# Cross attention 1: who copies the turned weights out of PSUM

## The reference, cut to what matters

```python
x = _layernorm(x + _L1_attn_ref(x, ...))        # state = tanh(state * exp(A) + Bu[t]), 1024 steps; y = states @ C_w.T + ...
x = _layernorm(x + _L1_xattn_ref(x, ctx_768, Wq, Wk, Wv, Wo, bo))

def _L1_xattn_ref(x, context, Wq, Wk, Wv, Wo, bo):   # 16 heads of 64, 77 keys per sequence
    q, k, v = (x @ Wq), (context @ Wk), (context @ Wv)          # split into heads
    attn = softmax(einsum('bqhd,bkhd->bhqk', q, k) / sqrt(64))
    return einsum('bhqk,bkhd->bqhd', attn, v).reshape(B, Nq, 1024) @ Wo + bo
```

## Time and profile before

| what | us |
|---|---|
| runs | 2312.34, 2312.98, 2318.16; median 2312.98 |
| the profiled execution's own time | 2315.36 |
| its span | 2313.6 |
| PE busy over the span | 1758.1 (76%) |
| DVE busy | 1782.5 (77%) |
| ACT busy | 1333.4 (58%) |
| POOL busy | 847.5 (37%) |
| the 11-transpose groups L1675 of the stage | first at 1644.4, last at 1990.1 |

### The profile page before, as it was taken

One profiled execution on the slowest core, in us unless ns is written; L12 is line 12 of the kernel. 1 busy time (PEld: TensorE's weight loads), 2 busy tenths in 40 slices (PEclk: granted clock), 3 DMA queues, 4 the chain that ended last, 5 costly groups with the idle time before them and its releaser, 6 DMA issues. The chain is left out here.

```text
span 2313.6 us, 36269 instructions
## 1 busy us (share of the span) xinstructions
PE 1758.1 (76%) x12104; PEld 1097.3 (47%) x12104; DVE 1782.5 (77%) x4542; ACT 1333.4 (58%) x3347; POOL 847.5 (37%) x983
## 2 busy tenths in 40 slices
PE   8939999999968777775666666665899999556564
PEld 4503333333336566664444554434577667433333
DVE  4668888888626888885888888845578787599997
ACT  1204666666733344342078888899999992144443
POOL 2420000000007768753333333300575775323232
PEclk9957999999967989896777777767899999866766
DMA  2001111111020010000000000010000000000000
GB/s 79 19 21 29 30 30 30 30 28 29 12 63 15 12 31 13 12 6 19 1 19 1 1 1 1 1 35 23 1 19 1 1 1 1 30 12 16 14 15 18
DMA packets 42807, 41.54 MB, mean 18 GB/s; under 512 B 16054, under 2 KB 34670, under 8 KB 42622
## 3 DMA queue, kind: packets, MB, share of 16 engines
q1 hardware_dynamic: 42622, 39.23, 6.4%
HBM read 22.03 MB, written 4.19 MB: 11 GB/s over the span
## 5 line engine op out<-in xcount | busy, mean ns | idle before, releaser
L763 ACT ACTIVATE ST<-ST,aexp 128x1 f32<-128x1 f32 x2046 | 581.9, 384 | 2.0 <-PEq L57 2.0
L597 ACT ACTIVATE PT<-PS 128x512 f32<-128x512 f32 x576 | 309.8, 597 | 219.5 <-PE PS L482 188.6
L558 DVE CUSTOM_DVE_ANT_0 junk<-PS,maskw 128x128 bf16<-128x128 f32 (+3 forms) x512 | 226.5, 486 | 33.8 <-PE PS L459 33.8
L459 PE MATMUL PS<-KT,QT 48*128 48x512 bf16 (+3 forms) x768 | 190.1, 351 | 54.1 <-DMA QT<-QS 33.0
L561 DVE TENSOR_REDUCE MX<-PS 128x1 f32<-128x512 f32 x256 | 164.6, 685 | 27.7 <-PE PS L459 24.9
L501 PE MATMUL PS<-PT,VP 128*32 128x256 f32 (+1 forms) x2560 | 184.2, 370 | 0.0
L94 PE MATMUL PS<-ident,X 128*128 128x128 f32 x256 | 64.0, 339 | 143.7 <-DVE X L128 129.6
L631 POOL TENSOR_SCALAR nm<-MX 128x16 f32<-128x16 f32 x32 | 6.5, 203 | 431.1 <-DVE MX L564 431.1
L1663 PE MATMUL PS<-L_xattn_VW,l_pT 112*128 112x256 f32 x704 | 157.4, 379 | 2.9 <-issue 2.9
L459 PEld LDWEIGHTS PS<-KT,QT 48*128 48x128 bf16 x768 | 58.4, 94 | 200.0 <-issue 80.3
L1648 PE MATMUL PS<-Q,l_xT 128*128 128x512 f32 (+1 forms) x384 | 144.1, 526 | 1.7 <-DVE l_s L1696 1.7
(11 more groups left out here) (317 smaller groups left out, 4502.5 us busy)
## 6 DMA issues: line engine op xcount, KB each, us to landing
KT<-KS SPq DMA_DIRECT2D x192, 32.0 KB, 2.0
QT<-QS SPq DMA_DIRECT2D x192, 32.0 KB, 2.0
xs<-in_x SPq DMA_DIRECT2D x8, 512.0 KB
cx<-in_x SPq DMA_DIRECT2D x32, 128.0 KB, 2.0
out<-j_xn SPq DMA_DIRECT2D x32, 128.0 KB, 1.7
QT<-NMT SPq DMA_DIRECT2D x192, 2.0 KB
f_raw<-in_L_ffn_w SPq DMA_DIRECT2D x2, 1024.0 KB, 5.5
j_raw<-in_L_ffn_w SPq DMA_DIRECT2D x2, 1024.0 KB, 5.3
```

Source lines behind the costliest of these rows:

```text
L459: T.matmul(bank(u % 3)[:, 0:w * P], QT[i % R][rows, qt * P:(qt + 1) * P], KT[i % R][rows, k0 * P:(k0 + w) * P], start=True, stop=True).the ...
L558: V.tensor_tensor_reduce(junk[u % 3][:, 0:w * P], bank(u % 3)[:, 0:w * P], maskw[:, BANK - w * P:], 1.0, NEG, ALU.add, ALU.max, MX[i % 2][ ...
L597: C.activation(PT[n % 4][:, 2 * pr + e, 0:w], bank(3 + u % 3)[:, 0:w], ACT.Exp, scale=0.25).then_inc(e_done, 1)
L763: C.activation(self.ST[:, m, t:t + 1], self.ST[:, m, t - 1:t] if t else self.zero[:, :], ACT.Tanh, bias=self.BU[:, m, t:t + 1], scale=self ...
```

## The change

ACT's copy keeps the first eight of the 11 pieces (1024 of 1408 columns, banks 4 and 5). The last three (384 columns, bank 6) are copied by DVE, in the next slot, between L1684 and L1687. The transposes signal twice: `d_ptr` after the eighth, `d_ptr1` after the last. The product L1663 waits for both copies (`d_pT`, `d_pT1`), and so do the next tile's transposes; the subtraction that writes `s` again waits for `d_ptr1` instead of `d_ptr`.

```diff
                 if on(o):
                     T.wait_ge(d_pT, o + 1)
+                    T.wait_ge(d_pT1, o + 1)
...
                     T.wait_ge(d_p, p + 1)
                     if p >= 1:
                         T.wait_ge(d_pT, p)
+                        T.wait_ge(d_pT1, p)
                     for i in range(VN):
                         last = T.transpose(PS[0:VR, 4 * BANK + i * P:4 * BANK + (i + 1) * P], s[p % 3][:, i * VR:(i + 1) * VR], ident[:, :])
-                    last.then_inc(d_ptr, 1)
+                        if i == 7:
+                            last.then_inc(d_ptr, 1)
+                    last.then_inc(d_ptr1, 1)
...
                     V.tensor_add(X[:, c, :], bank(3)[:, D:2 * D], X[:, c, :]).then_inc(i_y, 1)
+                if on(o):
+                    V.wait_ge(d_ptr1, o + 1)
+                    if o >= 2:
+                        V.wait_ge(d_mm, o - 1)
+                    V.tensor_copy(pT[o % 2][:, 8 * P:VN * P], PS[0:VR, 6 * BANK:6 * BANK + (VN - 8) * P]).then_inc(d_pT1, 1)
                 if on(p):
...
                     if sc >= 3:
-                        V.wait_ge(d_ptr, sc - 2)
+                        V.wait_ge(d_ptr1, sc - 2)
...
                     C.wait_ge(d_ptr, p + 1)
                     if p >= 2:
                         C.wait_ge(d_mm, p - 1)
-                    C.copy(pT[p % 2][:, :], PS[0:VR, 4 * BANK:4 * BANK + VN * P]).then_inc(d_pT, 1)
+                    C.copy(pT[p % 2][:, 0:8 * P], PS[0:VR, 4 * BANK:4 * BANK + 8 * P]).then_inc(d_pT, 1)
```

More of the change, by code:

```diff
@@ L1601, in cross_layer1 @@
         i_mm, i_xb, i_y, i_xn = st.sems("i_mm i_xb i_y i_xn")
-        d_tr, d_xT, d_xb, d_sc, d_mx, d_sub, d_exp, d_den, d_rden, d_p, d_ptr, d_pT, d_mm, d_y, d_xn = st.sems(
-            "d_tr d_xT d_xb d_sc d_mx d_sub d_exp d_den d_rden d_p d_ptr d_pT d_mm d_y d_xn")
+        d_tr, d_xT, d_xb, d_sc, d_mx, d_sub, d_exp, d_den, d_rden, d_p, d_ptr, d_ptr1, d_pT, d_pT1, d_mm, d_y, d_xn = st.sems(
+            "d_tr d_xT d_xb d_sc d_mx d_sub d_exp d_den d_rden d_p d_ptr d_ptr1 d_pT d_pT1 d_mm d_y d_xn")
         nI, nD = Norm(st, ctx, "nI", D), Norm(st, ctx, "nE", D)
```

## The result

| | before | after |
|---|---|---|
| median of 15 runs each, same chip | 2314.34 us (2312.34 to 2319.46) | 2320.27 us (2316.77 to 2324.40) |
| ratio after / before, 95% interval | | 1.0023 (1.0015 to 1.0030) |
| the profiled execution's own time, its span | 2315.36, 2313.6 | 2319.92, 2318.2 |

The change costs 0.23%, some 5.3 us (2314.34 x 0.0023). That is within 0.3%, as the prediction gave it 92 in 100, but it is a real loss, since the interval leaves out 1, and the median lies 1.3 us above the range's upper end of 2319. Of the 6.2 us between the forecast of 2314.1 and 2320.3, 1.4 is that the kernel before has a median of 2314.34 over 15 runs and not the 2312.98 of the first three. The rest is the change's.

A forecast was written before the change was run, and what follows sets the result against it. The prediction took PE's 11.14 us slot as the bound, lengthened by POOL in places. Full slots 0, waits +0.3 and tail +0.8 made +1.1 us, so 2312.98 became 2314.1 us, range 2309 to 2319.

The forecast's parts named there:

- The bound: Full slots: PE's 11.14 us slot sets the pace, not ACT at 99.8% busy; shortening ACT's copy gains 0.
- rival B: Full slots: ACT is the bound after all, so its shorter copy gives 2307.2 or 2302.7 us; 4 in 100.
- DVE's copy: DVE in the full slots: each new copy takes 0.55 us, hidden in its wait for the scores; cost 0.
- Rival C: Full slots: DVE's slot becomes the longest if POOL holds the copy, for example 2325 us; 3 in 100.
- The waits: PE's 62 additional satisfied waits: 0.005 us each, 0.3 us in all, bounds 0 and 3.9.
- The last two products: Stage's end: products wait for DVE's copies, starting 0.4 and 0.8 us later; +0.8 us to the end, bounds 0 and 0.9.
- rival E: Stage's end: the tail doesn't lengthen and the change does nothing at all, 2313.0 us; 20 in 100.
- The sum: Whole kernel: 0 in full slots, +0.3 for waits, +0.8 in the tail, +1.1 us in all.
- my likeliest case: Whole kernel: the forecast's own case, spanning 2312.3 to 2317.7 us with waits from 0 to 3.9; 66 in 100.

The follow-up runs named there:

- e5: Kernel before with ten more satisfied waits on PE ahead of each product but the first, 310 in all; 2316.91 us, ratio 0.9998.
- e7: Kernel after without PE's two waits for the copies ahead of the transposes; 2319.84 us, ratio 1.0012 to the kernel before.
- e11: Kernel after with PE's two waits for the copies ahead of the transposes replaced by two repeated waits for d_p; 2321.00 us, ratio 1.0018.
- e6: Kernel before with each of PE's two waits a tile for the copy written twice; 2317.87 us, ratio 0.9996.
- e4: Kernel before with the split for the last two tiles only, DVE copying in the same slot behind the norm's statistics; 2315.70 us, ratio 0.9996.
- e3: Kernel after with 14 added identity transposes on PE ahead of each of the last two products; 2319.01 us, ratio 1.0014 to the kernel before.
- e1: Kernel after with the last two tiles copied whole by ACT again; 2318.89 us, ratio 1.0006 to the kernel before.
- e2: Kernel after with the split kept for the last two tiles alone; 2319.14 us, ratio 1.0011 to the kernel before.
- e9: Kernel after with the split kept for the last tile only, ACT copying 31 tiles whole; 2319.62 us, ratio 1.0012 to the kernel before.
- e0: Kernel after run again without any edit; 2320.10 us, ratio 1.0017 to the kernel before.

## Why the prediction was right and wrong

**The bound.** Right: PE's slot is 11.13 us (11.14 before) and its waits are 3.2. ACT's copy took 1.01 us (1.02 expected). Its saving bought nothing, so rival B is out. Its waits for the transposes did not become more and longer as I wrote (15.2 to 12.3 us, 13 times both): ACT idles elsewhere, ahead of its exponential.

**DVE's copy.** Right: 0.547 us against 0.55. L1692's waits shrank by 13.8 us, where 15 were due. No copy was held: all 32 lie beside work of POOL, which had begun before the copy in 16 of them, and they took between 541 and 553 ns. In the POOL-bound stretch the wait for the scores fell to 0.25 us from 0.72, and nothing behind it moved. Rival C is out. The Trainium skill (SBUF — State Buffer, Who interferes with whom) lets a VectorE copy meet GpSimd where it can use both ports, and that an operand in PSUM rules this out stands in another of its pages (VectorE: DVE Perf Modes, Why PSUM operands drop a tier). These 32 durations agree; had the copies been held, some would have been longer by up to one of POOL's small operations.

**The waits.** Taken as 0.3 us with 3.9 as the bound; `e5` gives 0.005 us each at most and no change of the slot. The size was harmless. The sum had no term at all for what lies behind the stage. There 31 semaphore instructions of PE, through with their waits long before, brought 1.3 us at the next stage's first load: `e7` and `e11` show that. That it goes by the fetch of instructions is only argued from the packet.

**The last two products.** This is the step that failed most. The place of the copy was right: the copy stands behind L128 and the last products wait for it; rival E is out. The term was mis-sized: +0.8, measured +1.11 up to the product's start. I took 0.10 us from a copy's end to the product, as with one wait for a copy. In the kernel after it is 0.25 (1986.07 to 1986.32, 1994.28 to 1994.54), and it counts twice, since tile 31's order hangs on tile 30's product: 0.40 + 0.15 and 0.80 + 0.30. `e6` has the same 0.15 from a second wait alone, so the second wait, which I had costed for the full slots only, explains the 0.3. `e4` fits: the wait for DVE's copy stands first there too, and the product starts 0.25 us behind DVE's copy, though only 0.13 behind ACT's, whose wait stands in the second instruction. And `e3`, where no semaphore instruction stands between the wait for DVE's copy and the product, has just the 0.8 us. Worse, I ended the step at the product's start, with "+0.8 us goes to the end", as if the product behind a longer gap kept its length. It took 1.69 us more, as the granted clock fell in it. With `e1`, `e2`, `e3` and `e9` this is shown in the traces: the fall comes with the longer gap and goes with the filler.

**The sum.** Forecast 0 + 0.3 + 0.8 = 1.1. Measured 0 in the slots, 0 for the waits as such, 2.8 in the tail and 1.3 at the load: 4.1, and 4.6 in the one trace with 0.46 of scatter ahead of it. In ratios, 0.0012 and 0.0006 make 0.0018; after, `e0` and `e11` gave 1.0023, 1.0017 and 1.0018, the kernels with the tail alone 1.0011, 1.0012 and 1.0012, the one with the load alone 1.0006, `e3` with the load and 0.8 us of tail 1.0014, and the five with neither 0.9996 to 1.0004. All agree within their intervals. The range's upper end took in 3.9 us for the waits and nothing for what hangs on a longer gap, and it was put on a median of three runs. The lower end of my likeliest case, 2312.3, doesn't follow from its terms either: with nothing for waits and tail they give 2313.0. That the loss stayed within 0.3%, as forecast, owes much to how wide that is: 6.9 us. The sum had 1.1 of the some 5 us in it.

## What to carry to other kernels

When work moves to "the head of the next slot", read the drain of the pipeline by itself: the slot's cover is gone there and the copy meets whatever the engine still has ahead of it. And where a gap ahead of a PE group at the end of a stage grows, don't end the sum at the group's start: look whether the granted clock holds through the group. An engine that is busy 99.8% may still not be the bound; who waits for whom, and the slot's length, decide.

## What the runs showed of the hardware

In this kernel a gap of 2.03 us in place of 1.47 ahead of the last product brought the granted clock from 1.00 to 0.50 for some 3.4 us inside it: 0.56 us of lateness cost 1.7 more. 310 satisfied waits on a PE without idle time changed neither slot nor time, but a semaphore instruction more behind the one that PE stood at cost 0.15 us. And in the changed kernel 31 semaphore instructions more on PE, with either of two sets of semaphores, made a burst of loads some 10 us behind the stage's last product 1.3 us longer, with a packet of instructions in it; in the kernel before (`e6`) as many did not.
